# First weight strips by another queue, a reordered third set, output banks and feed-forward loads, and 64 matmuls ahead of all others

## The reference

```
xn = layernorm(x)
q, kv = xn @ W_q.T, xn @ W_kv.T            # split in 16 heads of 128
qf, kvf = fft(q), fft(kv)                  # along the 128 of a head, each
qf, kvf = qf/|qf|, kvf/|kvf|               # divided by its length
kvf = cumsum(kvf, over tokens)
v = ifft(qf * kvf).real ; a = v @ W_o.T
x1 = x + layernorm(a)
h = layernorm(x1)
f = h @ W.T + b + sum over the two best of 8 experts of gate * (h @ A_e.T) @ B_e.T
out = x1 + layernorm(f)
```

## Time and profile before

| what | value |
|---|---|
| median of 3 runs | 1017.05 us (1016.85 to 1020.64) |
| the profiled execution | 1017.06 us |
| its span, core 6 (the slowest) | 1015.1 us |
| spans of the other cores | 1008.6 to 1013.8 us |
| TensorE busy | 979.7 us, 97% of the span |
| VectorE, ScalarE, GpSimd busy | 588.5, 342.4, 54.8 us |
| DMA | 112.22 MB, mean 111 GB/s |

### The profile page before, as it was taken

How to read it: one execution, slowest core, us unless ns; L and a number is a source line. 1 busy time by engine, 2 the same in 40 slices (tenths; PEclk the granted TensorE clock), 3 DMA queues, 4 the chain that set the end, 5 groups by cost and what they waited for, 6 DMA issues and landing times.

```text
span 1015.1 us, 14019 instructions; the slowest of 8 cores (1008.6 to 1015.1 us)
## 1 busy us (share of the span) xinstructions
PE 979.7 (97%) x5072; PEld 468.3 (46%) x5072; DVE 588.5 (58%) x846; ACT 342.4 (34%) x573; POOL 54.8 (5%) x106
## 2 busy tenths in 40 slices
PE   3989999999999999999999999999998999999996
PEld 2444444444444444444444444444444444444442
DVE  3134765455554456555467777666675656557565
ACT  5256666766667755656330000000000000000001
POOL 5000000000000000000001000000100000000000
PEclk9999999999999999999999999999998999999999
DMA  9995545565565222220085878877985233132222
GB/s 133 168 164 91 87 86 110 104 108 87 87 115 104 63 42 42 42 37 7 21 296 116 174 153 154 155 149 147 175 155 176 77 111 123 65 125 97 91 104 83
DMA packets 65667, 112.22 MB, mean 111 GB/s; under 512 B 37184, under 2 KB 45376, under 8 KB 63040
## 3 DMA queue, kind: packets, MB, share of 16 engines
q0 software_dynamic: 14688, 51.42, 32.9%
q1 hardware_dynamic: 50912, 59.91, 19.3%
HBM read 120.79 MB, written 33.55 MB: 152 GB/s over the span
## 4 chain that ended last, share of the span: by engine, by line
PE 89%; DMA 6%; DVE 2%; issue 1%; ACT 1%; DVEq 1%; SPq 0%; POOL 0%; ACTq 0%; POOLq 0%
PE PS L357 40%; PE PS L634 21%; PE PS L819 20%; DMA XT<-xt 4%; PE PS L291 3%; PE PS L771 1%; PE PS L315 1%; PE PS L826 1%; PE PS L396 1%; DMA XT<-wos 1%; DMA XT<-bias 1%; DMA WK<-wkv 1%; ACT WK L258 0%; DVEq L81 0%; SPq L695 0%
## 5 line engine op out<-in xcount | busy, mean ns | idle before, releaser
L357 PE MATMUL PS<-XT,WK 128*128 128x512 bf16 x2048 | 482.6, 380 | 3.2 <-DMA XT<-xt 3.2
L357 PEld LDWEIGHTS PS<-XT,WK 128*128 128x128 bf16 x2048 | 196.1, 98 | 220.0 <-issue 5.8
L634 PE MATMUL PS<-XT,VH 128*128 128x512 bf16 x1024 | 221.5, 379 | 1.3 <-DMA XT<-wos 1.3
L819 PE MATMUL PS<-WK,VH 128*128 128x512 bf16 x896 | 205.1, 381 | 0.0
L634 PEld LDWEIGHTS PS<-XT,VH 128*128 128x128 bf16 x1024 | 100.1, 98 | 122.3 <-issue 1.7
L819 PEld LDWEIGHTS PS<-WK,VH 128*128 128x128 bf16 x896 | 86.9, 98 | 101.3 <-issue 2.1
L389 DVE TENSOR_TENSOR WK<-WK 128x1024 bf16<-128x1024 bf16 x60 | 41.5, 692 | 151.6 <-ACT WK L381 147.6
L646 ACT ACTIVATE SM<-SM 128x1 f32<-128x1 f32 x48 | 14.2, 295 | 270.0 <-DVE SM L682 108.0
L273 ACT ACTIVATE WK<-PS 128x512 bf16<-128x512 f32 x120 | 70.4, 592 | 61.8 <-PE PS L291 60.4
L835 DVE TENSOR_TENSOR XT<-PS,XT 128x1024 f32<-128x1024 f32 x31 | 38.0, 1224 | 57.7 <-PE PS L802 51.2
L381 ACT ACTIVATE WK<-PS 128x1024 bf16<-128x1024 f32 x60 | 61.4, 1024 | 29.1 <-PE PS L357 25.7
(11 more groups left out here) (77 smaller groups left out, 600.0 us busy)
## 6 DMA issues: line engine op xcount, KB each, us to landing
out<-XT SPq DMA_DIRECT2D x15, 1024.0 KB, 4.8
WK<-wkv POOLq DMA_DIRECT2D x16, 512.0 KB, 6.4
WK<-wq POOLq DMA_DIRECT2D x16, 512.0 KB, 6.2
WK<-wot POOLq DMA_DIRECT2D x16, 512.0 KB, 8.4
wos<-VH SPq DMA_DIRECT2D x32, 256.0 KB, 8.6
XT<-wos SPq DMA_DIRECT2D x4, 2048.0 KB, 9.9
WK<-x POOLq DMA_DIRECT2D x16, 512.0 KB, 7.9
x1s<-WK SPq DMA_DIRECT2D x16, 512.0 KB, 4.6
```

Source lines behind the costliest of these rows:

```text
L357: return e.matmul(bank(bk + r), WF[s % 3][:, c * 256 + r * 128:c * 256 + (r + 1) * 128], XT[:, b * 8192 + c * 512:b * 8192 + (c + 1) * 512 ...
L634: return e.matmul(bank(bk), VH[:, c * 2048 + t * 128:c * 2048 + (t + 1) * 128], XT[:, nn * 8192 + c * 512:nn * 8192 + (c + 1) * 512], star ...
L819: pe.do(lambda e, c=c: e.matmul(bank(bk), VH[:, c * 2048 + t * 128:c * 2048 + (t + 1) * 128], wchunk(c, nn * 512, (nn + 1) * 512), start=( ...
```

## The change

Five things are changed. (1) The four first strips are loaded by sp's queue as f32, without a cast, into RAWF (a part of VH that is not yet used), and `center` reads them there and writes bf16 to RAW. Pool waits for the third strip (`first[2]`) before it issues XT blocks 0 and 1. (2) 64 matmuls of PHIT with itself into bank 7, which nothing reads, stand first in TensorE's list. (3) Third set: its second strip is loaded after XT block 2, not before it; it is centred in block 3 after piece 1 and folded from piece 2 on. (4) Output: (1, 0) comes before (0, 3). (5) Feed-forward: W chunks 14, 15, the bias and three x1 tiles are issued before tile 15's norms in the lists, and `lora_turn(1)` stands before `ffn_half(0, 0)`.

```diff
--- before.py
+++ after.py
@@ -128,6 +128,7 @@
     WK = nc.alloc_sbuf_tensor("WK", [128, 39936], BF16)
     XTF = XT.bitcast(F32)
     WKF = WK.bitcast(F32)
+    VHF = VH.bitcast(F32)
 
     PHIT = nc.alloc_sbuf_tensor("PHIT", [HD, HD], BF16)
     PSI = nc.alloc_sbuf_tensor("PSI", [HD, HD], BF16)
@@ -141,6 +142,7 @@
     KT = WK[:, 20480:24576]
     QT = WK[:, 24576:28672]
     KT2 = VH[:, 10 * 2048:12 * 2048]
+    RAWF = [VHF[:, i * 2048:(i + 1) * 2048] for i in range(4)]
     KC = WK[:, 28672:32768]
     SQ2 = [WK[:, 32768 + i * 1536:32768 + i * 1536 + 1024] for i in range(2)]
     SQS = [WK[:, 33792 + i * 1536:33792 + i * 1536 + 512] for i in range(2)]
@@ -223,6 +225,12 @@
     raw_landed = {}
     raw_free = [None] * 4
 
+
+    l_first = [Landing(nc, "first%d" % i) for i in range(4)]
+    for k, (_, s, a) in enumerate(raw_jobs[:4]):
+        src = wkv_d if s == 0 else wq_d
+        raw_landed[raw_jobs[k]] = l_first[k].start(sp, RAWF[k], src.ap()[a * 128:(a + 1) * 128, :])
+
     def raw_load(job):
         kind, s, a = job
         i = raw_slot[job]
@@ -255,7 +263,8 @@
         k = ncent[0] % 2
         ncent[0] += 1
         act.wait(raw_landed[job])
-        t_sum = act.mark(lambda e: e.activation(RAW[i], RAW[i], AF.Identity, accum_out=SUM[k]))
+        src = RAWF[i] if job in raw_jobs[:4] else RAW[i]
+        t_sum = act.mark(lambda e: e.activation(RAW[i], src, AF.Identity, accum_out=SUM[k]))
         dve.wait(t_sum)
         dve.do(lambda e: e.tensor_scalar_mul(NMEAN[k], SUM[k], -1.0 / D))
         dve.drain()
@@ -466,20 +475,24 @@
             for fn, p, k in pieces.pop(0):
                 fn(p, k)
 
-    for job in raw_jobs[:4]:
-        raw_load(job)
+    first = raw_jobs[:4]
+    pool.wait(raw_landed[first[2]])
     for b in range(2):
         xt_load(b)
 
-    first = raw_jobs[:4]
+    pe.wait(t_phit)
+    for _ in range(64):
+        pe.do(lambda e: e.matmul(bank(7, 0, 128), PHIT[:, :], PHIT[:, :], start=True, stop=True))
+
+
     center(first[0])
     for k, job in enumerate(first[:3]):
         center(first[k + 1])
         for g in range(4):
             fold_w(job, g, act if g % 2 == 0 else dve)
     raw_load(("w", 2, 0))
+    xt_load(2)
     raw_load(("w", 2, 1))
-    xt_load(2)
     xt_load(3)
     sp.wait(xt_landed[0][-1])
     t_bones = l_const[1].start(sp, BONES[:, :], bones_d.ap())
@@ -514,17 +527,19 @@
             normalize(i0 - 2)
         for k in range(1, n):
             part(i0, k)
-            if strips:
+            if k > 1 and strips:
                 strips.pop(0)()
             part(i1, k - 1)
-            if strips:
+            if k > 1 and strips:
                 strips.pop(0)()
             if b >= 1 and k == 1:
                 norm(i1 - 2)
                 invert(i1 - 2)
                 normalize(i1 - 2)
-            if b == 2 and k >= 2:
-                center(("w", 2, k - 2))
+            if b == 2 and k == 3:
+                center(("w", 2, 0))
+            if b == 3 and k == 1:
+                center(("w", 2, 1))
         evacuate(i0)
         square(i0)
         if b == 2:
@@ -695,6 +710,18 @@
         sp.do(lambda e: e.dma_start_transpose(dst, XN).then_inc(l_xnt.sem, 16))
         xnt_ready[t] = (l_xnt.name, l_xnt.sem, l_xnt.count)
 
+
+    l_bias = Landing(nc, "bias")
+    l_x1r = [Landing(nc, "x1r%d" % i) for i in range(3)]
+    l_out = [Landing(nc, "out%d" % i) for i in range(3)]
+    x1r_landed = {}
+    x1r_free = [None] * 3
+    out_stored = [None] * 3
+
+    def x1r_load(t):
+        sp.wait(x1_stored[t], x1r_free[t % 3])
+        x1r_landed[t] = l_x1r[t % 3].start(sp, X1R[t % 3], x1s_d.ap()[t * 128:(t + 1) * 128, :])
+
     early = list(range(14))
     late = [14, 15]
     every = list(range(16))
@@ -707,7 +734,7 @@
     queue_pieces(last)
     while pieces:
         long_piece()
-    for t, nn in ((0, 1), (0, 2), (0, 3), (1, 0)):
+    for t, nn in ((0, 1), (0, 2), (1, 0), (0, 3)):
         out_mm(t, nn, early)
     pool.wait(vh_ready[15], slot_done[last], norm_tok[last % 2], inv_tok[last])
     x_load(0)
@@ -733,32 +760,18 @@
             t_agw = l_agw.start(pool, AGW, agw_d.ap())
         if t == 15:
             t_bbt = l_bbt.start(pool, BBT, bbt_d.ap())
+
+            pool.wait(y_tok[(15, 3)])
+            w_load(14)
+            w_load(15)
+            sp.wait(y_tok[(15, 3)])
+            t_bias = l_bias.start(sp, BIAS, bias_d.ap())
+            for k in range(3):
+                x1r_load(k)
         attn_norm(t)
         next_norm(t)
         if t + 1 < NT and t >= 1:
             x_load(t + 1)
-    t_out = y_tok[(15, 3)]
-
-
-    l_bias = Landing(nc, "bias")
-    l_x1r = [Landing(nc, "x1r%d" % i) for i in range(3)]
-    l_out = [Landing(nc, "out%d" % i) for i in range(3)]
-    pool.wait(t_out)
-    w_load(14)
-    w_load(15)
-    sp.wait(t_out)
-    t_bias = l_bias.start(sp, BIAS, bias_d.ap())
-    x1r_landed = {}
-    x1r_free = [None] * 3
-    out_stored = [None] * 3
-
-    def x1r_load(t):
-        sp.wait(x1_stored[t], x1r_free[t % 3])
-        x1r_landed[t] = l_x1r[t % 3].start(sp, X1R[t % 3], x1s_d.ap()[t * 128:(t + 1) * 128, :])
-
-    for t in range(3):
-        x1r_load(t)
-
     xat_ready = {}
     xat_mm = {}
 
@@ -901,11 +914,11 @@
     ffn_mm(1, 0, every)
     for nn in range(4):
         lora_mm(0, nn)
+    lora_turn(1)
     ffn_half(0, 0)
     ffn_half(0, 1)
     ffn_norm(0)
     x1r_load(3)
-    lora_turn(1)
     for t in range(1, NT):
         for nn in range(4):
             if t == 1:
```

## The result

The changed kernel is slower: a median of 1024.8 us against 1017.0 us for the kernel before; the ratio is 1.007, 95% interval 1.0051 to 1.0088, that is 7 us. The forecast was 1010.6 us. Some executions, three of the first nine of the changed kernel (1100 us and more), show one die at a lower clock, and all medians and ratios given here leave them out. The profiled execution took 1024.71 us and has a span of 1022.9 us on core 3.

What follows compares the result with a forecast made beforehand. TensorE, busy 97% of the span, was taken as the bound, so only its idle and low-clock time could be won: -2.8 + 1.5 - 1.3 - 3.9 = -6.5 us, from 1017.06 to 1010.6 us, range 1005.5 to 1014.7.

Steps and rivals of the forecast that it cites:

- All three signs: Prediction wrong if strips land over 3.4 us apart, XT's flow breaks after the fourth strip, or wt wait passes 4 us.
- The start: First 95 us: earlier strips and XT, less the new stall, end block 3 at 84.5, a gain of 2.8 us (1 to 4).
- With some crowding it lands at 6.6: Start: first strip by sp, issued at about 1.5 us, lands at 6.6, from a 4.8 us transfer by sp.
- I take 2.9: Start: each 1 MB strip without a cast costs 2.9 us, between bounds of 2.5 and 3.4.
- The stall of 3.0 us at the second strip: Block 3, third set: TensorE stands 3.0 us before the second strip's first group, hanging on its own norm.
- Behind it wait only further matmuls: Block 3: after the second strip's new stall nothing else is delayed; no further wait was priced.
- The clock: Clock falling to half rate behind the new block 3 stall: costs 1.5 us (0 to 3.4).
- The warm-up: Start: the 64 matmuls may lift the clock early but are worth nothing by themselves; bounds 0 and 1 us.
- The banks: Output stage: putting (1, 0) first covers the wait for W_o's fourth piece; gain 1.3 us on core 6 (0 to 1.3).
- Feed-forward, "-3.9 us": Feed-forward: 7.0 us won at the L805 wait, less 2.1 for the tile 2 transpose and 1.0 for W chunk 15.
- The third rival: Start: uncast strips cost 6.3 us each, projections start 10 us later than now, total 1019; chance 4%.
- The second rival: Feed-forward bias makes W chunk 15 4.5 us late, or clock falls the full 3.4 us: 1014.1 or 1012.5; chance 22%.

Runs made afterwards that it cites:

- start_alone: The kernel before with only strips by sp as f32, XT behind the third strip and the 64 matmuls; ratio 1.0016 to the kernel before.
- third_alone: The kernel before with only the third set's second strip loaded, centred and folded later; ratio 1.0025 to the kernel before.
- fill_waits: The changed kernel with 48, 40 and 40 unread PHIT matmuls put where TensorE waits; ratio 1.0044 to the kernel before.
- part5_alone: The kernel before with only the feed-forward change: early W chunks, bias and x1 tiles, lora_turn(1) ahead; ratio 1.0024 to the kernel before.
- loads_back: The changed kernel with bias and three x1 tiles issued behind tile 15's norms again; ratio 1.0029 to the kernel before.
- ffn_fixed: The kernel before with output banks, lora_turn(1) ahead, earlier W chunks and bias, tile 0's last VectorE steps deferred; ratio 0.9948 to the kernel before.

## Why the prediction was wrong

The sum was -6.5 us and the result +7. All three signs by which it called itself wrong came: strips more than 3.4 us apart, a break in XT's flow, and a wait for wt above 4 us (core 7). The steps, in its order:

1. **The start, "2.8 us won" (with the third set).** Wrong, the first step that failed. "With some crowding it lands at 6.6", of the first strip: it landed at 8.1 to 9.5 on the eight cores (8.95 on core 3). The 4.8 us behind that figure were of sp's stores of the output late in the run, not of loads at the start. "I take 2.9" us a strip, by the row of plain loads at 412 GB/s: measured 3.6 and 3.4 us (9.03, 12.64, 16.01), the upper bound and a little over. "Pool starts XT once the third has landed, at 12.4": it was 16.54, where 2.4 us of the delay are the first strip's, 1.2 us the pace of the next two and 0.6 us pass until pool issues. "The engines hardly idle": on core 3 their share was 0.34 from 17 to 18 us and 0.00 from 18 to 19, and XT's first piece was there only at 23.6, 7 us after its issue. The start itself lost 1.6 us (start_alone; not clear of nothing) where the loads should have won. BONES, which waits for XT block 0, was in no term of the sum.
2. **The stall of 3.0 us at the second strip.** Right to 0.1 us (2.86), and so is where it hangs. But it was booked as paid out of a gain that wasn't there.
3. **A wait left out.** "Behind it wait only further matmuls" was wrong. The prediction followed the strip's first group to its end, not the last group's. The fold that ends one part later makes `norm(i0)` wait 1.4 us on all cores. This was to be had from the code: what a moved step is followed by on ScalarE. Together with the stall and its falls of the clock the third part costs 2.5 us (third_alone).
4. **The clock.** In the sum stood 1.5 us for one place, half of what a fall had cost in the earlier trace rows. On core 3 there are three falls: behind the strip (8 matmuls in 3.05), behind W chunk 15, behind the tile 2 transpose (4.87 for 3.19, 1.7 us), each 1.5 to 1.7 us. fill_waits gives 2.6 us back by keeping TensorE busy and nothing else. The two in the feed-forward had been priced as waits alone. The Trainium skill (TensorE: Matmul & The Clock Gate, Part 1) says that idling takes the array back to half rate, and at all three on core 3 it did. But with stalls of 2.65 to 2.86 us at the strip on all eight cores only cores 0, 3 and 6 fell to half rate, so the length of the wait alone doesn't decide it.
5. **The warm-up.** Right in worth (nothing that can be seen), half right in how: the clock rose, and was down again on every core (from 10.8 to 13.8 us on) before the first projection.
6. **The banks.** Right in mechanism (no wait for wos), 0.4 us and not 1.3, with an interval that holds both.
7. **Feed-forward, "-3.9 us".** Wrong too, and the largest miss, 6.3 us: the part costs 2.4 us alone (part5_alone). L805 went as said. The tile 2 wait was 2.5 for 2.1. W chunk 15 was 3.6 us late on core 3 and 4.2 on core 7 (0.6 at the least, on core 1), not 1.0: of the bounds 0 and 4.5 the row of an even share was taken, and the measured one is near the other end. loads_back shows what was in front of it: the bias and the x1 tiles. To both waits come falls of the clock, which the -3.9 held at nothing.

The third rival ("paid by bytes written", the one on the slow side) was not it; strips cost 3.6 us, not 6. The second rival had the mechanism of chunk 15, by itself. The other side came of several waits of 1.4 to 3.7 us together, which no rival held; the parts measured alone, 1.6 + 2.5 - 0.4 + 2.4, give 6.1 of the 7 us. What stays open is how far the rest is chance: with intervals of 1.5 us it can't be told. Why sp's transposes now and then take over 20 us at 553 to 563 us was not tried.

## What to carry to other kernels

Follow every moved step to its last instruction on each engine, and ask what stands behind that one; a step that is one part later costs at its end too. A wait of 2.5 to 4 us on an otherwise dense TensorE is to be priced with a fall of the clock on some core, since the slowest of eight counts: in the changed kernel every core had at least one behind such a wait. Loads that are wanted late should not be issued beside those that are wanted next: here 2.6 MB of bias and x1 held up half a MB that TensorE needed within 13 us. Issuing the bias and x1 later took that wait away (loads_back), and so did issuing the W chunks 10 us sooner, when their place came free (ffn_fixed); which of the two is worth more was not run apart. A mean clock is not to be compared between kernels without asking where the record begins.

## What was not expected of the hardware

A 1 MB strip without a cast by sp took 3.4 to 3.6 us, the same as a cast one by pool, with 279 GB/s moved from 9 to 12 us on core 3; the 412 GB/s of late in the run did not hold there, and why is not shown; core 3 came near it only from 15 to 17 us (377 and 393 GB/s). After XT had been held back, its first piece landed 3.8 to 7.6 us after issue on the eight cores, 7.0 on core 3. And in the output stage one transpose by sp, issued at 555 to 563 us, took 16.2 to 17.7 us to land on all eight cores of the changed kernel, with no wait of TensorE; where it took over 20 us in other runs, TensorE mostly waited for VectorE later (2.0 us at 22.2, 3.5 us at 21.7).
